# A graph network's edge sums: one two-tensor comparison in place of two one-tensor comparisons

## What is computed

```python
# layer 0 (GCN), loops added to the edges
norm = dinv[src] * dinv[dst]
out = segment_sum(norm[:, None] * (x @ W)[src], dst, N) + b
x = layernorm(x + out + t_emb @ Wt + bt)

# layers 1 and 2 (SAGE), with a ReLU between them
summed = segment_sum(x[src], dst, N)
mean = summed / maximum(cnt, 1.0)[:, None]
h = mean @ Wl.T + x @ Wr.T + b
# at the end: x = layernorm(x + h)
```

## Time and profile before

| | |
|---|---|
| median of 3 runs | 3669.8 us (3665.4 to 4489.6) |
| the profiled execution | 3676.9 us, span from first to last instruction 3674.9 us |
| busy: PE, DVE, ACT, POOL | 3181.8, 1919.1, 1050.7, 2435.1 us |
| DMA | 744 MB, 202 GB/s over the span |
| mean granted TensorE clock | 0.945 |

### The profile page before, as it was taken

How to read it: one execution, slowest core, us unless ns; L and a number is a source line. 1 busy time by engine, 2 the same in 40 slices (tenths; PEclk the granted TensorE clock), 3 DMA queues, 4 the chain that set the end, 5 groups by cost and what they waited for, 6 DMA issues and landing times.

```text
span 3674.9 us, 73564 instructions
## 1 busy us (share of the span) xinstructions
PE 3181.8 (87%) x9570; PEld 1625.4 (44%) x9571; DVE 1919.1 (52%) x5738; ACT 1050.7 (29%) x1526; POOL 2435.1 (66%) x2365
## 2 busy tenths in 40 slices
PE   7378889999999799999888889968889888888887
PEld 7133444444444344444444444434444444444444
DVE  8333344454444355554655666635455456555665
ACT  0311112222222222223333333322222233333343
POOL 0377777777666376665777777646656567777674
PEclk9788999999999899999989999989999998889999
DMA  4777777777766566666777777766655567766664
GB/s 157 251 207 211 212 218 231 231 239 230 217 211 203 169 201 190 189 176 192 209 223 227 226 228 236 223 186 196 200 168 176 166 179 207 207 177 197 189 198 145
DMA packets 257091, 744.01 MB, mean 202 GB/s; under 512 B 44188, under 2 KB 45758, under 8 KB 256792
## 3 DMA queue, kind: packets, MB, share of 16 engines
q0 software_dynamic: 187680, 615.14, 58.1%
q10 hardware_dynamic: 57276, 105.62, 8.1%
q1 hardware_dynamic: 11868, 20.99, 1.7%
HBM read 688.67 MB, written 53.71 MB: 202 GB/s over the span
## 4 chain that ended last, share of the span: by engine, by line
PE 55%; issue 17%; DMA 9%; POOL 7%; ACTq 3%; ACT 3%; DVE 2%; DVEq 2%; POOLq 0%; SPq 0%
PE sum_ps L891 33%; PE prod_ps L898 10%; DMA raw<-table,idx_ring 8%; PE root_ps L898 7%; POOL raw L373 7%; DVE raw L609 1%; ACTq L210 1%; ACT hi L746 1%; PE aggT_ps L871 1%; PE sum_ps L859 1%; DVEq L210 1%; PE root_ps L906 1%; PE selfT_ps L913 1%; ACTq L214 1%; DMA selfbuf<-table 1%
## 5 line engine op out<-in xcount | busy, mean ns | idle before, releaser
L373 POOL DMA_INDIRECT raw<-table,idx_ring x2346 | 2419.6, 1031 | 1113.1 <-issue 685.3
L891 PE MATMUL sum_ps<-raw,oh 128*128 128x512 f32 x3528 | 1520.7, 558 | 57.3 <-issue 36.1
L609 DVE TENSOR_TENSOR raw<-raw,hi 128x256 fp32r<-128x256 f32 x2352 | 840.9, 420 | 610.0 <-ACT hi L746 609.5
L746 ACT ACTIVATE hi<-raw 128x1024 fp32r<-128x1024 f32 x588 | 619.6, 1057 | 1733.3 <-SPq L297 1408.7
L574 DVE TENSOR_SCALAR oh<-iota_row,tile_base,dst_tab 128x128 fp32r<-128x128 bf16 x2352 | 717.5, 354 | 687.8 <-issue 473.5
L891 PEld LDWEIGHTS sum_ps<-raw,oh 128*128 128x128 f32 x3528 | 676.0, 198 | 592.1 <-issue 523.4
L891 PE MATMUL sum_ps<-hi,oh 128*128 128x512 f32 x1176 | 520.1, 524 | 251.5 <-DVE raw L609 192.5
L898 PE MATMUL prod_ps<-W,aggT 128*128 128x512 f32 x1176 | 547.5, 609 | 17.0 <-ACT aggT L671 16.6
L891 PEld LDWEIGHTS sum_ps<-hi,oh 128*128 128x128 f32 x1176 | 208.9, 196 | 486.1 <-issue 480.5
L898 PE MATMUL root_ps<-W,selfT 128*128 128x512 f32 x800 | 393.5, 637 | 0.0
L898 PEld LDWEIGHTS prod_ps<-W,aggT 128*128 128x128 f32 x1176 | 222.0, 194 | 277.2 <-issue 269.3
(11 more groups left out here) (125 smaller groups left out, 1199.8 us busy)
## 6 DMA issues: line engine op xcount, KB each, us to landing
selfbuf<-table ACTq DMA_DIRECT2D x152, 256.0 KB
raw<-table,idx_ring POOLq DMA_INDIRECT x2346, 3.8
table<-stage ACTq DMA_DIRECT2D x7, 1792.0 KB, 6.7
table<-X ACTq DMA_DIRECT2D x49, 256.0 KB, 4.2
table<-hbuf ACTq DMA_DIRECT2D x49, 256.0 KB
X<-table ACTq DMA_DIRECT2D x49, 256.0 KB
X<-in_x SPq DMA_DIRECT2D x6, 2048.0 KB
out<-X ACTq DMA_DIRECT2D x48, 256.0 KB
```

What stands on the lines that cost most here:

```text
L373: nc.gpsimd.indirect_dma_start(out=raw[:, n, j, :], out_offset=None, in_=tables[L][:, :], in_offset=bass.IndirectOffsetOnAxis(ap=idx_ring[ ...
L609: last = v.tensor_tensor(lo[:, n, j, cols], raw[:, n, j, cols], hi[:, k, j, cols].bitcast(fp32), ALU.subtract)
L746: a.activation(hi[:, k, :, :], raw[:, n, :, :], ACT.Copy).then_inc(S["hi_ready"], 1)
L891: last = mm(bank, of[:, j, :], half[:, j, :], start=fresh, stop=False, skip_group_check=True)
```

## The change

The helper `one_hot` (one chunk) becomes `one_hots` (both chunks of a group). Instead of two TENSOR_SCALARs with 128 columns, one bf16 tensor and two per-partition numbers each, DVE runs one SCALAR_TENSOR_TENSOR with 2 x 128 columns. It reads `iota_row` repeated for both chunks, one per-partition number (`tile_base`) and a second tensor, `dst_tab`, of which each of two numbers is repeated 128 times. The result is the same, in the same place. Waits and semaphores stay as they were.

```diff
-                def one_hot(to, chunk, tile):
-
-                    v_out = v.tensor_scalar(to, iota_row[:, :], tile_base[:, bass.ds(tile, 1)],
-                                            dst_tab[:, bass.ds(chunk, 1)], ALU.add, ALU.is_equal)
-                    return v_out
+                def one_hots(to, g, tile):
+
+                    return v.scalar_tensor_tensor(to, iota_row[:, :].unsqueeze(1).to_broadcast([P, CH, P]),
+                                                  tile_base[:, bass.ds(tile, 1)],
+                                                  dst_tab[:, bass.ds(g * CH, CH)].unsqueeze(2).to_broadcast([P, CH, P]),
+                                                  ALU.add, ALU.is_equal)
 
                 def tile_end(g, t1):
 
                     dve.wait_ge(S["next_used"], t1 + T * L)
-                    one_hot(oh_next[:, 0, :], g * CH, t1)
-                    one_hot(oh_next[:, 1, :], g * CH + 1, t1).then_inc(S["next_made"], 1)
+                    one_hots(oh_next[:, :, :], g, t1).then_inc(S["next_made"], 1)
...
                         dve.wait_ge(S["pe_done"], g + (NG * L + 1))
-                        one_hot(oh[:, n, 0, :], g * CH, first)
-                        last = one_hot(oh[:, n, 1, :], g * CH + 1, first)
+                        last = one_hots(oh[:, n, :, :], g, first)
```

## The result

| | before | after |
|---|---|---|
| median of the comparison | 3669.1 us (4 runs, 3665.4 to 4489.6) | 3766.9 us (4 runs, 3764.7 to 3772.3) |
| span of the profiled execution | 3674.9 us | 3762.7 us |
| layer 0, 1, 2, from weight load to weight load | 1080.7, 1177.4, 1269.9 us | 1087.5, 1158.9, 1368.9 us |

The changed kernel takes 1.0272 times as long, interval 1.0252 to 1.0292: slower by 2.7%. One run of the kernel before, a slow one of 4489.6 us, is left out of the ratio. The forecast was 3735 us in a range of 3660 to 3800.

The account below looks back on a forecast made before the run. Gather issue on POOL was taken to set the pace in some stretches, PE or layer handovers in others. Holds of 86 us, less 11 for bursts made waited and 10 of gain, gave +65: 3735 us, range 3660 to 3800.

Parts of the forecast that it names:

- DVE's time: One-hots on DVE: the new instruction takes about 478 ns, 0.12 us less per pair, plus 0.06 us less address work.
- The new one-hot alone holds a gather: A gather's issue on POOL is held by the new instruction by itself, costing POOL 0.037 to 0.051 us per instruction.
- A: Stretch 150 to 700 us, layer 0: gather issue sets the pace, so all 12 us of holds reach the end.
- B: Stretch 700 to 1240 us: PE sets the pace and hides about 9 us of holds, so 0 reaches the end.
- Joined to a burst: Subtractions following one-hots without a wait (direct burst): the new instruction lengthens their hold on gathers by 0.29 us per burst.
- C and D: Stretches 1240 to 1750 us (layer 1 begins) and 1750 to 2350: 6 and 35 us of holds reach the end.
- E and F: Stretches 2350 to 2950 us (layer 2 begins) and 2950 to 3640: 6 and 27 us of holds reach the end.
- PE's waits for DVE: PE's 95 waits for DVE's subtractions and one-hots shorten, 17 us at most; 10 us of gain taken.
- Not held at all: Rival: the repeated number is fetched at once, so gathers aren't held and only the gain is left; 3660 us, chance 0.12.
- Faster: Rival: DVE is the late one at direct bursts, each group gains 0.18 us, 70 us in all; 3600 us, chance 0.05.
- Never joined: Rival: the one-hot holds gathers but releases POOL before the burst; +27 us, 3697 us, chance 0.22.
- Held without a break: Rival: burst, one-hot and burst become one hold, 0.58 us instead of 0.29; +133 us, 3803 us, chance 0.15.

Follow-up runs that it names:

- a_pad12: The changed kernel with twelve never-run instructions ahead of DVE's layer-2 loop, moving it 16 places; 1.0112, 1.0132 and 1.0108 of the kernel before.
- b_pad150: The kernel before with 150 never-run instructions ahead of DVE's layer-2 loop, moving it 154 places; 1.0017 of the kernel before.

## Why the prediction was right in its number and wrong in its reasons

**DVE's time: right.** 478 ns were forecast, 484 and 477 measured (1176 and 147 instructions); DVE's busy time fell by 161 us, and 175 were forecast. Of the address steps 1,176 went, 2499 to 1323, but those left take 86 ns in the median for 57: all of them together took 178.2 us before and take 108.0 now, a saving of 70 us for the forecast 1323 x 0.06 = 79.

**The new one-hot alone holds a gather: right, at about half the size.** Sorted as before, 345 gathers start under a one-hot and take 0.104 us too long on average, 35.7 us in all; before it were 537 with 0.018 and 9.4 us. In A, where nothing else changed, POOL's excess (busy less 0.945 us per gather) is 416.9 - 426 x 0.945 = 14.4 us for 7.7 before, 6.7 more, where the forecast had 12; in B it is 1.2 more (11.3 for 10.1), where it had 9. So the term was taken at least twice too large. Layer 0 grew by 6.8 us, which fits the 6.7 in A passing whole, but it isn't shown: on one of the later chips layer 0 is 6.0 us longer with the new one-hot too (a_pad12 beside b_pad150), although POOL's excess in it is 20 us for 37. And with only 1.2 us in B, that PE hides such a hold wasn't tested.

The Trainium skill, "SBUF — State Buffer", section "Who interferes with whom", has a GpSimd instruction that reads SBUF contend with a DVE one of two SBUF inputs, but infers that a gather's descriptor generation is let off; the 0.104 us under this instruction, as the 2.23 us in the earlier trace rows, go against the second part.

**Joined to a burst: wrong, with the wrong sign.** This was the step that carried the sum: +0.29 us for each direct burst, 58 of the 86 us that were to reach the end. Measured: the gathers that meet a direct burst in layers 1 and 2 had 0.538 us too much before (294 gathers, 158 us) and have 0.177 after (249, 44 us). Where 148 of them were held by over half a microsecond, 18 are. An example of after (timeline):

```profile
3100.67 1.42 DVE L608 TENSOR_TENSOR raw<-raw,hi 128x256 fp32r<-128x256 f32 x4
3100.69 1.22 POOL L373 DMA_INDIRECT raw<-table,idx_ring  x1 [0.30 <-issue]
```

It starts 0.02 us into a burst, as in the earlier trace rows, and is held by 0.28 instead of 1.29 us: released within the burst, as after a wait. Of the gathers that start in the first 0.9 us of a direct burst and are held, 158 of 167 come free only at its end before, and 19 of 156 after. Over the whole kernel POOL's excess fell from 203 to 111 us, where 140 more were forecast; the mean gather, which was to rise from 1031 to 1091 ns, fell to 992. I had modelled the hold as lasting as long as instructions of one kind follow each other, from bursts which all had the same pair of instructions ahead; the rows of before showed the length of the hold for that one neighbour only, and the model put the neighbour's length in and left its kind out. The lower bound of the term was 0, and the truth lay under it: the 0.455 us of a direct burst itself was open to change, and the bounds had taken it as given. In C and D 8 more gathers start, and layer 1 is 18.5 us shorter (41 us longer forecast). That the shorter holds did this is likely there, not shown: on a later chip layer 1 takes 1400.9 us with the new one-hot and 1400.5 with the old (a_pad12, b_pad150), with an excess of 43 us for 90.

**What reaches the end.** For E and F 33 us were forecast from holds; layer 2 lost 99, and none of it comes from a longer hold (excess in F 67.6 before, 418.35 - 418 x 0.945 = 23.3 after). The missing term, which the forecast put at nothing by leaving it out, is the code: DVE loses 24 places per loop, its layer-2 loop comes to lie where each jump back stalls, and 48 x (3.76 + 2.47) us, 300 us, of DVE's time go with 99 at the end, a third; the rest, as I read it, falls into DVE's slack between groups. The trace of before had all it took for the rival: the same stall in ACT's loop, 3.73 us of "issue" behind L765, and q14 with 258 packets, five per round. I had read the chain's "issue 17%" and asked nothing of it. The sum of the parts is then 6.8 - 18.5 + 99.0 = 87.3 us, against 87.8 between the spans. That this lies near the 65 forecast is chance: layers 1 and 2 were wrong by 60 and 66 us with opposite signs.

The Trainium skill, "Runtime: NRT & Kernel Launch", section "Instruction fetch mechanics", says that a taken branch whose target lies outside the two pages of code held by an engine has to fetch it first. The stall behind the jumps agrees in kind, 3.76 us here. Its pages are 256 instructions; here packets of 8,192 bytes, 128 instructions, move, and a loop of 312 instructions doesn't stall at one place and does 79 places on, so the length alone doesn't decide.

**PE's waits for DVE.** 10 us of gain were forecast from 95 shorter waits. In layer 1, where no stall of DVE is in the way, these waits didn't shorten: 39.4 us before, 39.8 after. In layer 2 the stall took them from 64.4 to 187.7. So the trace doesn't show the gain.

**The rivals.** "Not held at all" is ruled out by the 0.104 us under the one-hot. "Faster" had DVE's shorter path worth 60 us; in layer 1, where no stall hides it, at most 18.5 came of it. "Never joined" comes nearest in what POOL does, but it too kept the old bursts as they were. "Held without a break" forecast 3803 us, 36 above what was measured and so about as near as the forecast (32 below), by a hold that went the other way. None of the rivals was about the place of the code.

**What stays open.** What the change is worth without the stall on a chip where the kernel before takes 3670 us wasn't timed. Adding up layers 0 and 1 gives -12 us, and layer 2 unknown; on the slower chips it was no gain in any pair of kernels with the same loops moved. Whether the shorter holds are worth anything, why the seams open, and the exact rule for the place of a loop stay open too.

## What to carry to other kernels

A change that adds or takes away instructions moves every loop behind it in its engine's code. So before its effect is put down to the new instruction, compare the instruction queue's packets and the time from each loop's last branch to the next instruction, per layer or copy of the loop; a few instructions that never run, put ahead of the loop, tell place and change apart in one experiment. Read them in the kernel before too, in every engine: here the fastest version, by 0.7 and 0.5%, is the kernel before with a loop of ACT moved by 64 places, and the only other one that beat it has that loop moved too. And the price of a contention measured with one neighbour isn't its price with another.

## What the hardware showed that I had not expected

- A jump back over a loop of 284 to 312 instructions costs 0.2 to 0.3 us or 3.1 to 3.8 (medians), on DVE with a second gap of 2.1 to 2.5 us some steps later, by nothing but the loop's place in the code; each such round loads 5 packets of 8,192 bytes.
- A gather's hold under four subtractions of 256 columns depends on what ran ahead of them: 0.51 to 0.61 us on average after two 128-column TENSOR_SCALARs, 0.36 to 0.39 after one of these and one SCALAR_TENSOR_TENSOR in either order, 0.15 to 0.18 after a single SCALAR_TENSOR_TENSOR of 256.
- A SCALAR_TENSOR_TENSOR of 256 columns takes 484 ns, whose second tensor is a number repeated 128 times twice; one of 128 columns with such an operand takes 350 ns, like the TENSOR_SCALAR (354). A second tensor that is only a repeated number holds gathers all the same, by 0.104 us on average; the one of 128 columns by 0.03 to 0.06.
- The chips of the experiments took 16 to 18% longer for the same kernel. The steps on DVE's queue took 131 to 146 ns in the mean there and 101 to 105 on the first chip, single register steps up to 1.4 us for 0.21, while DVE's, ACT's and POOL's own operations kept their durations (484, 1056, 986 ns for 484, 1056, 992 with the new one-hot).
